# A decoder layer on one core: GpSimd instead of ScalarE makes the decay stage's two rectifications of positive sign

## The reference

```python
# attention: 32 query heads of 8, 8 key/value heads
scores = einsum('bhqd,bhkd->bhqk', Q, K) / sqrt(8)
out = softmax(scores) @ V
x = layernorm(x + out @ Wo + bo)
# decay stage (WKV): per channel, over time, k = x, v = ctx
no = maximum(o, u + kt); A = exp(o - no); E = exp(u + kt - no)
y = (A * p + E * vt) / (A * q + E)
no2 = maximum(w + o, kt); A2 = exp(w + o - no2); E2 = exp(kt - no2)
p, q, o = A2 * p + E2 * vt, A2 * q + E2, no2
x = layernorm(x + y)
# feed-forward
h = square(relu(x @ up_w))                 # 256 -> 1024
moe = (x @ expert_weight) * sum(top_k(x @ gate_w, 2))
x = layernorm(x + layernorm(h @ down_w + moe) * gamma + beta)
```

## Time and profile before

| | us |
|---|---|
| median of 3 runs | 206.65 |
| lowest, highest | 206.05, 209.31 |
| the profiled execution's time | 206.2 |
| its span, first instruction to last | 204.3 |
| mean granted clock of PE | 0.994 |

### The profile page before, as it was taken

One profiled execution on the slowest core, in us unless ns is written; L12 is line 12 of the kernel. 1 busy time (PEld: TensorE's weight loads), 2 busy tenths in 40 slices (PEclk: granted clock), 3 DMA queues, 4 the chain that ended last, 5 costly groups with the idle time before them and its releaser, 6 DMA issues.

```text
span 204.3 us, 4342 instructions
## 1 busy us (share of the span) xinstructions
PE 190.2 (93%) x1315; PEld 112.2 (55%) x1315; DVE 164.3 (80%) x390; ACT 154.0 (75%) x336; POOL 118.7 (58%) x231
## 2 busy tenths in 40 slices
PE   7999799989998999999999999999999999999960
PEld 3754343334433334847476466564655687898940
DVE  7778787888889999977989887978974588777373
ACT  6660378877999889979899898979998984773530
POOL 8005409992886723757257845886469569663722
PEclk9999999999999999999999999999999999999997
DMA  6026213874332117200230000000020000000011
GB/s 200 31 57 177 58 32 75 241 218 84 115 79 71 47 26 249 74 5 0 58 93 6 2 11 0 6 5 6 2 83 29 0 0 26 5 26 0 17 37 51
DMA packets 13414, 11.76 MB, mean 58 GB/s; under 512 B 3664, under 2 KB 11344, under 8 KB 13136
## 3 DMA queue, kind: packets, MB, share of 16 engines
q1 hardware_dynamic: 13248, 11.35, 19.4%
q10 hardware_dynamic: 144, 0.13, 0.2%
HBM read 6.57 MB, written 1.05 MB: 37 GB/s over the span
## 4 chain that ended last, share of the span: by engine, by line
PE 69%; DVE 17%; DMA 5%; issue 4%; ACT 2%; POOL 1%; POOLq 0%; DVEq 0%; ACTq 0%
PE ps_b L877 12%; PE ps_heads L690 12%; PE ps_b L860 8%; DVE maxima L1281 8%; PE ps_exp L674 7%; PE ps_max L661 6%; DMA q_rows<-max_t 5%; PE ps_a L818 4%; PE ps_exp L860 4%; PE ps_a L769 3%; PE ps_b L843 3%; PE ps_heads L877 2%; PE ps_a L756 1%; DVE top L1370 1%; PE ps_a L641 1%
## 5 line engine op out<-in xcount | busy, mean ns | idle before, releaser
L1281 DVE TENSOR_REDUCE maxima<-ps_max 128x2 f32<-128x512 f32 x128 | 82.4, 682 | 13.5 <-PE ps_max L661 13.3
L911 ACT ACTIVATE probs<-ps_exp 128x512 f32<-128x512 f32 x128 | 70.9, 598 | 14.9 <-PE ps_exp L674 13.5
L661 PE MATMUL ps_max<-k_rows,q_rows 64*128 64x256 bf16 x256 | 40.0, 272 | 2.2 <-DVE maxima L1281 1.4
L674 PE MATMUL ps_exp<-q_rows,k_rows 64*128 64x512 bf16 x128 | 38.6, 383 | 1.9 <-DMA q_rows<-max_t 1.2
L690 PE MATMUL ps_heads<-probs,v_cols 128*32 128x512 f32 x256 | 33.5, 603 | 0.0
L1157 POOL TENSOR_TENSOR rstd<-var_eps,minus_half 128x1 f32<-128x1 f32 x32 | 18.7, 586 | 23.3 <-DVE var_eps L1249 23.3
L661 PEld LDWEIGHTS ps_max<-k_rows,q_rows 64*128 64x128 bf16 x256 | 14.1, 94 | 27.6 <-DVE maxima L1281 18.5
L877 PE MATMUL ps_b<-down_sb,inner_t 128*128 128x256 f32 x112 | 27.1, 382 | 0.0
L860 PE MATMUL ps_b<-x_t,up_sb 128*128 128x128 f32 x192 | 24.4, 278 | 0.6 <-ACT x_t L886 0.4
L860 PEld LDWEIGHTS ps_b<-x_t,up_sb 128*128 128x128 f32 x192 | 22.7, 192 | 2.4 <-ACT relu_t L1039 1.4
L877 PEld LDWEIGHTS ps_b<-down_sb,inner_t 128*128 128x128 f32 x112 | 20.1, 190 | 2.6 <-ACT relu_t L1039 0.2
(11 more groups left out here) (152 smaller groups left out, 344.0 us busy)
## 6 DMA issues: line engine op xcount, KB each, us to landing
q_rows<-q_parts SPq DMA_DIRECT2D x42, 64.0 KB, 2.1
x_t<-in_x_cols SPq DMA_DIRECT2D x4, 256.0 KB, 3.6
x_in<-in_x SPq DMA_DIRECT2D x4, 256.0 KB, 4.0
ctx_t<-in_ctx_cols SPq DMA_DIRECT2D x4, 256.0 KB, 4.3
up_sb<-in_up_w SPq DMA_DIRECT2D x1, 1024.0 KB, 7.2
down_sb<-in_down_w SPq DMA_DIRECT2D x1, 1024.0 KB, 5.4
out_y<-y_out SPq DMA_DIRECT2D x8, 128.0 KB, 1.7
post_sb<-in_w_post SPq DMA_DIRECT2D x1, 906.0 KB, 5.7
```

The lines of the kernel that those rows point to most:

```text
L661: last = nc.tensor.matmul(ps_max[n % 2][:, r, :], q_rows[b][at:at + HALF, g, REP * jj + 2 * half + r, h * P:h * P + P], k_rows[b][at:at + ...
L674: nc.tensor.matmul(ps_exp[n % 2][:, :], k_rows[b][at:at + HALF, JH * g + jj, kt * P:kt * P + P], q_rows[b][at:at + HALF, g, REP * jj:REP * ...
L911: nc.scalar.activation(probs[n % 8][:, :], ps_exp[n % 2][:, :], ACT.Exp, scale=SCALE).then_inc(s_exp, 1)
L1281: nc.vector.tensor_reduce(maxima[s % 2][:, g, j // JH, 0, at:at + 2], ps_max[n % 2][:, :, :], AX, ALU.max, negate=True).then_inc(s_max, 1)
```

## The change

The rectifications of positive sign, `re1` and `re3`, go from ACT's queue to POOL's, as `tensor_scalar` with a maximum against 0. ACT keeps `re0` and `re2`. A new pair of semaphores, `s_parg`, counts POOL's; `ex0` and `ex1` wait for both counts, and so does the next chunk's `delta`.

```diff
-                    for i, sign in ((0, -1.0), (1, 1.0)):
-                        if AT[f"re{i}"][p] == tick:
...
-                            nc.scalar.activation(wgt[:, i, :, cols], delta[:, :, cols], ACT.Relu,
-                                                 scale=sign).then_inc(s_arg[0], 1)
-                        if AT[f"re{2 + i}"][p] == tick:
...
-                            for c in range(CT):
-                                last = nc.scalar.activation(wgt[:, 2 + i, c, cols], delta[:, c, cols], ACT.Relu,
-                                                            scale=sign, bias=bonus_decay[:, i, c:c + 1])
...
+                        nc.scalar.activation(wgt[:, 0, :, cols], delta[:, :, cols], ACT.Relu,
+                                             scale=-1.0).then_inc(s_arg[0], 1)
...
+                            last = nc.scalar.activation(wgt[:, 2, c, cols], delta[:, c, cols], ACT.Relu,
+                                                        scale=-1.0, bias=bonus_decay[:, 0, c:c + 1])
...
-                            act.wait_ge(s_arg[half], 2 * p + 2)
+                            act.wait_ge(s_arg[half], p + 1)
+                            act.wait_ge(s_parg[half], p + 1)
...
+                    if AT["re1"][p] == tick:
+                        if p == 0:
+                            for g in range(NSET):
+                                gp.wait_ge(s_q3[g], 4)
+                        gp.wait_ge(s_delta, p + 1)
+                        if before(p):
+                            gp.wait_ge(s_y, before(p))
+                        gp.tensor_scalar(wgt[:, 1, :, cols], delta[:, :, cols], 0.0, None, ALU.max).then_inc(s_parg[0], 1)
+                    if AT["re3"][p] == tick:
+                        gp.wait_ge(s_delta, p + 1)
...
+                        for c in range(CT):
+                            last = gp.tensor_scalar(wgt[:, 3, c, cols], delta[:, c, cols], bonus_decay[:, 1, c:c + 1],
+                                                    0.0, ALU.add, ALU.max)
+                        last.then_inc(s_parg[1], 1)
```

```diff
                 if n is not None:
+                    if n == 0:
+                        for i in range(3):
+                            keep_busy(tick - 1)
                     exp_unit(n // UNITS, n % UNITS)
...
                     if n < 2 * UNITS:
+                        keep_busy(tick)
+                    if n >= 8 and tick + 1 not in SCORE_MAX:
                         keep_busy(tick)
```

The whole table `AT` is written anew. The order of steps within each engine stays much as it was; the ones that move most are these:

```diff
-        "load": (1, 2, 67, 78, 79, 190, 257, 335, 336, 545, 546, 561, 764, 1091),
-        "k": (3, 25, 91, 300),
+        "load": (1, 69, 70, 71, 127, 128, 378, 402, 495, 496, 557, 811, 812, 813),
+        "k": (2, 51, 99, 303),
...
-        "mc0": (89, 189, 298, 430, 530, 705, 863, 1004),
-        "mc1": (122, 239, 338, 492, 619, 788, 938, 1053),
+        "mc0": (76, 192, 304, 400, 551, 706, 878, 1014),
+        "mc1": (132, 243, 364, 459, 595, 760, 925, 1076),
...
-        "re2": (328, 568, 665, 733, 881, 1038, 1147, 1230),
-        "re3": (341, 567, 700, 750, 831, 1056, 1143, 1239),
-        "re0": (371, 518, 667, 721, 866, 1013, 1113, 1214),
-        "re1": (399, 531, 663, 720, 865, 1037, 1122, 1215),
+        "re0": (329, 536, 665, 726, 831, 1044, 1145, 1215),
+        "re3": (338, 520, 669, 787, 876, 1058, 1125, 1236),
+        "re2": (356, 560, 704, 764, 875, 1039, 1157, 1235),
+        "re1": (397, 512, 671, 716, 839, 1032, 1133, 1214),
```

## The result

The changed kernel takes 217.69 us in the median (216.76 to 218.51), the kernel before 206.35 us beside it (204.71 to 209.31). The ratio is 1.053, 95% interval 1.047 to 1.059. It is slower by 5.3%; 204.1 us was forecast, with a range of 201.0 to 208.0. The profiled execution took 217.97 us, with a span of 216.2 us against 204.3. A ratio compares fast executions alone, since the kernel before also has executions at a lower granted clock that take over 1.5% more than its fastest.

A forecast was written before the change was run, and what follows sets the result against it. It took DVE as the bound from 50 to 78 us, and PE, ACT and DVE queues close to full from 78 to 160. Terms -1.6 - 0.4 + 0.5 - 1.0 = -2.5 us from 206.65 gave 204.1 us, range 201.0 to 208.0.

The forecast's parts named there:

- 1.15 us a chunk, 9.2 us in all: POOL's new work: 0.45 us for `re1`, 0.35 for each half of `re3`; bounds 6.4 to 13.8 us in all.
- rival C: ACT is the true pace from 78 us on, so all 5.4 us show: 200.7 us; chance 0.14.
- POOL's own time costs nothing, as long as it stands ahead of nobody.: From 50 to 160 us POOL's waits of 7.9 and 5.4 us were to hide its new work: 0 us.
- Latency of the decay stage: `re0` and `re1` run side by side, so `ex0` could start some 0.3 us sooner; priced at nothing.
- 5.4 x 9.8 / 32.8 = 1.6 us: From 78 to 160 us, ACT's 5.4 us relief times the share of PEld's idle time ACT ends: 1.6 us gained.
- rival B: PE or DVE covers ACT's relief: 205.3 to 207 us, about 206.2; chance 0.22.
- The tail, 0.4 us.: Near 174.75 us, PE's wait for a relu behind ACT's two L986 shrinks: 0.4 us gained, bounds 0 and 0.47.
- The new order: 1.0 us: Near 39 us the max_t copy lands sooner because the up_sb load is issued later: 1.0 us gained, bounds 0 to 1.2.
- +0.5 us: POOL's new work slows DVE operations with two SBUF inputs: 0.5 us lost, bounds 0 and 1.5.
- Rival E: All 24 new POOL instructions meet two-input DVE operations, 10.3 us on DVE, half on the path: 208.9 us; chance 0.04.
- Dummy matmuls: 0: Nine more `keep_busy` matmuls stand ahead of waits: 0 us, at most 9 x 0.21 us.
- Rival D: POOL's queue holds the maxima parcels of groups 5 and 6 behind `re3`/`re1` of chunks 2 to 4: 210.3 us; chance 0.14.

The follow-up runs named there:

- e1: The changed kernel with its new order and dummy matmuls, but `re1` and `re3` made by ACT again; 207.35 us, ratio 1.0045 to the kernel before.
- e14: e12 with `re1` of chunk 0 moved earlier and `re1`, `re3` of chunk 4 moved later in POOL's queue; 209.42 us, ratio 1.009.
- e4: The changed kernel with `re3` of chunk 4 moved directly behind `re1` of chunk 4 in POOL's queue; 213.29 us, ratio 1.029.
- e10: The changed kernel with `re3` of chunk 4 early and POOL's `re1` and `re3` cut to one column per channel block; 208.50 us, ratio 1.007.
- e15: e14 with the positive rectifications of chunks 6 and 7 made by ACT; 208.81 us, ratio 1.008.
- e3: The changed kernel without the nine additional dummy matmuls; 216.04 us, ratio 1.042 to the kernel before.
- e5: The kernel before with fourteen POOL operations added at its start, where POOL is idle; the two forms took 0.87 and 0.72 us alone.
- e11: The kernel before, in its old order with its old dummy matmuls, with `re1` and `re3` made by DVE; 213.53 us, ratio 1.027.
- e9: The changed kernel, in its new order, with `re1` and `re3` made by DVE instead of POOL; 213.83 us, ratio 1.030.
- e12: e4 with POOL's `re1` and `re3` of chunks 2 and 4 moved behind the first maxima parcels of groups 5 and 6; 212.36 us, ratio 1.030.

## Why the prediction was wrong, point by point

- **"1.15 us a chunk, 9.2 us in all" on POOL.** Mis-sized by two: 0.85 for `re1` and 0.71 for each half of `re3` make 2.3 us a chunk and 18.4 in all. The rows of the groups:

```profile
L1183 POOL TENSOR_SCALAR wgt<-delta,bonus_decay 128x128 f32<-128x128 f32 x16 | 11.6, 734 | 1.8 <-DVE delta L1402 1.8
...
L1176 POOL TENSOR_SCALAR wgt<-delta 128x256 f32<-128x256 f32 x8 | 6.8, 852 | 2.5 <-DVE delta L1402 1.9 <-POOL y_num L1208 0.5
```

  On the other side, ACT's relief is 6.8 us against e1 (155.7 to 148.9), not 8.7. The price came from the cast in the earlier trace rows because of its one input, and my upper end was the two-input row; both are under what was measured. The row of the operation's own form was there too: a TENSOR_SCALAR of 128x1 at 300 ns. It says what such an instruction costs with almost no data, and I used it only as a lower bound (which makes 8.0 us in all, not the 6.4 that the sum gives; the terms of rival C make 200.35 us, not 200.7; neither moves the forecast).

- **"POOL's own time costs nothing, as long as it stands ahead of nobody."** This is the step that failed: the sum has 0 for POOL's queue. With the order the same, the move costs 4.9% (e1's 1.0045 to 1.053), about 10 us, and five other places give 4.4% of it back (e14), about 9 us. The condition in the sentence is nearly right, as e14 shows; what I did not do was to walk through the queue and see who stands behind each of the 16 steps. I compared sums (13.3 us of idle time in the earlier trace rows against 9.2 of new work). An idle total says nothing of an in-order queue: `re3` of chunk 4 stood behind a `pow1` with a wait of its own for DVE. ACT's exponential waited for `re3`, and the relu and all score exponentials stood behind it: 6.3 us from unit 96 to 104 in the changed kernel against e4, of which part is the lower clock after the stall. At its early place in e4, `re3` costs 1.5 us of this again between units 80 and 96 (23.7 us for 22.2), and e4's median is 4.4 us lower.

- **"Latency of the decay stage ... worth nothing."** I saw a gain of 0.3 us and priced it at 0. In fact the exponentials start later, not sooner: they wait 8.6 us for POOL in the changed kernel (L1007: 7.4 for `re3`, 1.2 for `re1`), where ACT's own rectifications had made them wait for nothing. ACT's queue had carried these steps in order for free; the move made a wait between two engines at 16 places.

- **"5.4 x 9.8 / 32.8 = 1.6 us" for ACT's relief.** Measured: nothing (e10 against e1). In e1, PEld's idle time ended by ACT's score exponentials is 5.5 + 2.1 us from 78 to 160 us; in e10, with 3.9 us less on ACT, 5.0 + 1.8, and the stretches above last equally long. These waits are short, at most 0.8 us, and belong to the handshake over two banks of `ps_exp`; a share of idle time is no share of the path. The chain's 2% for ACT, which I had argued away, fits this, and so does rival B for this term.

- **"The tail, 0.4 us."** It came out the other way. PE's wait for a relu in the earlier trace rows is gone from its place (186 us in the changed kernel). It is gone in e1 as well, where ACT runs both L991 in a row for 0.72 us, so the order took it away and not the move; and PE waits there for DVE's `x` instead. The move costs 0.7 us in the tail, in two pieces of 0.4 and 0.3 us. One begins with a wait for a relu, the other with the wait for that `x`:

```profile
176.84 1.16 PE L866 MATMUL ps_b<-x_t,up_sb 128*128 128x128 f32 x8 [0.51 <-ACT relu_t L1045]
...
188.17 0.41 PE L642 MATMUL ps_a<-ident,x 128*128 128x128 f32 x2 [1.28 <-DVE x L1278]
```

  In e15, where ACT makes the last two chunks, these two waits are 0.25 and 0.96 us. The second piece is a meeting of POOL and DVE. POOL's `re1` of chunk 7 pushes x_beta back in its queue, so that it runs beside DVE's `x`, which takes 0.73 us beside it and 0.41 us in e15 and e1:

```profile
186.33 0.85 POOL L1176 TENSOR_SCALAR wgt<-delta 128x256 f32<-128x256 f32 x1 [1.32 <-DVE delta L1402]
187.15 0.72 POOL L1239 TENSOR_TENSOR x_beta<-x,post_sb 128x256 f32<-128x256 f32 x1
187.29 0.73 DVE L1278 TENSOR_SCALAR x<-h,mean_var,rstd 128x256 f32<-128x256 f32 x1 [0.31 <-issue]
```

- **"The new order: 1.0 us" for the first max_t copies.** The copy did what was forecast, and no time came of it. With the load of up_sb gone from behind it, it lands in 1.9 us, where it had taken 3.08:

```profile
39.95 0.53 SPq L607 DMA_DIRECT2D q_rows<-max_t  x1
...
DMA to landing us min/median/max: 1.9/1.9/1.9
```

  But it is issued 0.6 us later (39.95 for 39.38), behind ACT's copy to max_t, which runs at 39.62 for 39.05. And PE had waited little for its landing in the kernel before (waits of PE from 36 to 46 us), which bounded the gain:

```profile
PE ps_exp L674 <- DMA q_rows<-max_t: 0.3, 1, 0.3
```

  The score unit behind the copy (24) starts at 42.5 us in both kernels. I had taken the difference in landing for time of PE; the whole order is worth +0.9 us of span in e1, inside the bounds I gave, with an interval of the ratio that holds no change.

- **"+0.5 us" for contention** has the right size. The ten groups of DVE with two SBUF inputs take 25.7 us in the changed kernel, 24.9 in e1 and 27.0 in e14, and DVE's own new_v took 894 ns against 429. How much of this reaches the span isn't shown, but for the 0.3 us in the tail, at a DVE operation that I hadn't counted. Rival E's size is excluded: 10.3 us on DVE were needed for it.

- **"Dummy matmuls: 0"** fits e3, within its interval.

- **Rival D** had the right kind, a wait behind POOL's in-order queue, the right place (`re3`/`re1` of chunks 2 to 4), and 0.14 of the chances. It named a victim that counts for little. The parcels of groups 5 and 6 were held (2.5 and 2.6 us later in e4 than in e1), and letting them through gave 1.0 us at group 5 and nothing at group 6; ACT's exponential and the products toward `y` decide. Its 210.3 us was too little by 7.4, and my range ended at 208.0, in the near third of its own.

Not explained to the end: e14's 1.8 us of span over e1. Its starts put 0.4 by unit 64, 0.4 more by unit 104, and 1.0 behind unit 127. From the start of unit 120 to the end e1 takes 51.9 us, e14 53.0 and e15 52.3, so 0.7 of the last 1.0 is POOL's work on chunks 6 and 7. Of the rest, no run tells POOL's queue from the 2.1 us more of DVE's two-input operations.

## What to carry to other kernels

When an operation moves to another in-order engine, its new place matters more than its length. For each moved step, list what stands ahead of it and what that waits for, and what stands behind its consumer on the consumer's queue: the same 18 us of work on POOL cost 5.3% at the places given and 0.9% at spare ones. And compare kernels by the time from one fixed piece of work to the next: two kernels can differ by nothing in one such stretch and by 6 us in the next, and that names the place. Sums of idle time can't show this, and a share of short handshake waits is no gain to be had from relieving an engine that the chain of waits doesn't name. Take the price of an unseen form from the row of the same form, even of another size, and measure it once by itself.

## What the runs showed of the hardware

- GpSimd's one-input TENSOR_SCALAR with a maximum takes 0.84 to 0.87 us for 128x256 and 0.72 us (median) for 128x128 with an added column, in use (after) and alone (e5). A copy of 128x256 takes 0.40 us, a two-input add 0.61. A 128x128 maximum alone took 0.72 and 0.53 us in its two runs, a product of 128x256 with a constant 0.87 and 0.85. The Trainium skill ("GPSIMD Engine Reference", 4.1 Engine selection) says that GpSimd is about half as fast as VectorE on two inputs, and on one input runs roughly at line rate. These rows do not bear the second half out for TENSOR_SCALAR: 0.85 us on GpSimd against 0.36 to 0.46 us on DVE (e11, e9) for the same 128x256.
- While PE stood idle for 3.75 us, its granted clock began to fall (0.86 from 128 to 132 us), and it was 0.50 (1.2 GHz) in the next 4 us, where eight matmuls took 2.08 instead of 1.06 us. So a wait of PE can cost more than its own length. The granted clock also fell at a place without such a stall, and not each time: from 62 to 66 us PE was busy 3.00 of 4 us in the changed kernel, 2.99 in e12 and 2.97 in e4, and in the next 4 us the granted clock was 0.57 in the first two and full in e4. An estimate of the price of this fall is 1.2 us, from units 48 to 64, which take 17.3 us in e12 and 16.1 in e4; so spans of single executions compare only so far.
- A TENSOR_SCALAR of DVE with one 128x256 input took 0.73 us beside a two-input TENSOR_TENSOR of POOL, and 0.41 us with POOL idle (after at 187.29 us; e1 at 176.60, e15 at 178.16). Here PE waited for it.
